# One head's weights moved to ScalarE in every second index unit, layernorm statistics moved to the ends of both attentions, and a wider ring of banks in the second attention

## What is computed

```python
x = x + attn_a(layernorm(x))   # 16 heads, low-rank keys and values, rope, causal, and a top-k index mask
x = x + ffn(layernorm(x))      # 8 routed experts, top 2, and one shared expert
x = x + attn_b(layernorm(x))   # 16 heads of 16, ALiBi, causal
x = x + ffn(layernorm(x))
```

```python
dots = relu(einsum('bqhd,bkhd->bhqk', qi, ki))
index_scores = einsum('bhqk,h->bqk', dots, idx_w)      # weights of the heads, one number each
mask = index_scores >= kth largest of the row          # k from the pooled input
```

## Time and profile before

| | us |
|---|---|
| median of 3 runs | 2647.25 |
| lowest, highest | 2645.97, 2653.23 |
| profiled execution | 2644.66 |
| its span, first to last instruction | 2642.8 |
| PE busy | 2301.2 (87%) |
| DVE busy | 1812.3 (69%) |
| ACT busy | 1667.3 (63%) |
| POOL busy | 721.4 (27%) |

### The profile page before, as it was taken

The page is one execution under the profiler, slowest core; times in us unless marked ns, Lnnn a source line. Parts: engine busy times, 40 slices in busy tenths (PEclk is TensorE's granted clock), DMA queues, the critical chain, the costliest instruction groups (busy, mean ns, idle before and its releaser), DMA issues. The chain is left out here.

```text
span 2642.8 us, 42209 instructions
## 1 busy us (share of the span) xinstructions
PE 2301.2 (87%) x12536; PEld 1570.9 (59%) x12536; DVE 1812.3 (69%) x4044; ACT 1667.3 (63%) x3045; POOL 721.4 (27%) x992
## 2 busy tenths in 40 slices
PE   6956595657999999999999999799589999997995
PEld 3633263346778777877787878465344544444663
DVE  4888788875777677767776777542559888864523
ACT  3779587955777777777777777423226777775232
POOL 0215411542321332133214432136231000000163
PEclk9978797878999999999999999899778999999998
DMA  1011102131000000000000000412360101000124
GB/s 50 1 40 64 64 1 74 56 128 45 22 13 9 26 21 13 9 26 21 13 13 21 21 1 1 129 43 85 108 171 30 50 2 49 2 2 4 53 86 146
DMA packets 77562, 113.17 MB, mean 43 GB/s; under 512 B 23860, under 2 KB 51860, under 8 KB 74644
## 3 DMA queue, kind: packets, MB, share of 16 engines
q1 hardware_dynamic: 66776, 89.55, 10.8%
q0 software_dynamic: 10560, 20.86, 2.6%
HBM read 67.25 MB, written 39.58 MB: 40 GB/s over the span
## 5 line engine op out<-in xcount | busy, mean ns | idle before, releaser
L1425 DVE TENSOR_TENSOR aa_pt_lo<-psum,aa_pt_hi 128x512 fp32r<-128x512 f32 x544 | 350.3, 685 | 82.8 <-ACT aa_pt_hi L1355 80.2
L1900 DVE TENSOR_REDUCE ab_part_max<-psum 128x1 f32<-128x512 f32 (+3 forms) x640 | 348.0, 603 | 68.6 <-PE psum L1746 66.5
L1355 ACT ACTIVATE aa_pt_hi<-psum 128x512 fp32r<-128x512 f32 x544 | 297.2, 597 | 116.1 <-PE psum L1285 113.2
L1412 DVE CUSTOM_DVE_ANT_0 aa_prob<-psum,bias 128x512 f32<-128x512 f32 (+2 forms) x480 | 278.5, 597 | 118.4 <-PE psum L1275 99.9
L1848 ACT ACTIVATE ab_prob<-psum 128x512 f32<-128x512 f32 (+3 forms) x640 | 290.8, 544 | 91.6 <-PE psum L1775 89.0
L1239 POOL TENSOR_TENSOR x<-aa_y_out,x 128x256 f32<-128x256 f32 x256 | 188.3, 735 | 354.9 <-ACT aa_y_out L1373 310.1
L1273 PE MATMUL psum<-ka_hi,aa_q_hi 128*128 128x512 f32 (+3 forms) x640 | 268.6, 420 | 10.9 <-POOL aa_q_lo L1207 8.0
L1285 PE MATMUL psum<-ident,aa_prob 128*128 128x128 f32 x1600 | 253.0, 274 | 5.9 <-issue 4.6
L1347 ACT ACTIVATE aa_prob<-aa_prob,aa_neg_max 128x128 f32<-128x128 f32 (+11 forms) x192 | 227.9, 1188 | 43.3 <-DVE aa_neg_max L1418 41.6
L1296 PE MATMUL psum<-aa_pt_hi,c_stack 128*128 128x512 f32 x544 | 233.9, 430 | 5.9 <-ACT aa_out_t L1362 4.3
L1275 PE MATMUL psum<-ka_hi,aa_q_lo 128*128 128x512 f32 (+3 forms) x640 | 236.9, 370 | 0.0
(11 more groups left out here) (346 smaller groups left out, 4710.1 us busy)
## 6 DMA issues: line engine op xcount, KB each, us to landing
q_rows<-ixt_q_out SPq DMA_DIRECT2D x64, 256.0 KB, 2.0
aa_q_row<-q_rows SPq DMA_DIRECT2D x64, 256.0 KB, 2.6
f_back<-done SPq DMA_DIRECT2D x16, 512.0 KB, 7.8
w<-in_w SPq DMA_DIRECT2D x6, 896.0 KB, 9.8
x<-in_hidden SPq DMA_DIRECT2D x2, 2048.0 KB, 11.5
b_q_stack<-stash_q_hi SPq DMA_DIRECT2D x12, 256.0 KB, 3.8
b_k_stack<-stash_k_hi SPq DMA_DIRECT2D x12, 256.0 KB, 4.4
ixt_wq_n<-in_Wq_nope_T SPq DMA_DIRECT2D x2, 1024.0 KB, 5.1
```

What stands on the lines that cost most here:

```text
L1355: nc.scalar.activation(pt_hi[(TB[t] + j) % RING][:], turn_bank[(TB[t] + j) % RING], ACT.Copy).then_inc(pt_hi_done, 1)
L1412: nc.vector.tensor_tensor_reduce(prob[t % 2][h][:, c * CH:c * CH + w], score_bank[(QB[t] + h * chunks[t] + c) % 2][:, 0:w], bias[:, TRI[t] ...
L1425: nc.vector.tensor_tensor(pt_lo[ring][:], turn_bank[(TB[t] + j) % RING], pt_hi[ring][:].bitcast(F32), ALU.subtract).then_inc(pt_lo_done, 1)
L1900: nc.vector.tensor_reduce(part_max[e % 2][:, at, part:part + 1], s_bank[piece % PIECES][:, 0:w], AX.X, ALU.max).then_inc(s_used, 1)
```

## The change

It has four parts.

In `index_scores`, odd units no longer multiply head 0 on DVE. ACT does it: after the relus of heads 0 and 1 it copies `relu[:, 0, :]`, scaled by the weight, into `scores`, and counts that in the new semaphore `weighed`. DVE starts an odd unit with head 1 and waits there for `weighed`. ACT's relu of head 0 in an even unit waits for its own copy (`weighed`) where it waited for DVE. Even units keep their form, and DVE's sums are counted 7 to a pair of units instead of 8.

At the end of `attention_a` DVE takes the statistics of each tile once POOL has added its last head, and the second layernorm gets them; it loses its own.

In `attention_b` the last transposed scores may use seven banks. Up to the last score nothing changes. From the first slot after it (`FREED`) the slots go round banks 0 to 6; PE waits at that slot until DVE has freed all score banks (`s_used`), and at each slot for what was last in its bank.

Also in `attention_b`, the sixteen reciprocals of the output tiles become one instruction over all tiles, in place, ahead of the first tile, and each tile's statistics are taken one step behind its addition. The fourth layernorm gets them.

```diff
+    DVE_SUMS = 2 * HI - 1
...
+        weighed = sem("weighed")
+
+        def sums(u, h):
+            return DVE_SUMS * (u // 2) + (HI if u % 2 else 1) + h
+
+        def into(u):
+            t, half = divmod(u, HALVES)
+            return scores[:, t, half * WIDE:(half + 1) * WIDE]
...
                 for u in range(UNITS):
                     for h in range(HI):
                         act.wait_ge(dotted, u * HI + h + 1)
-                        if u:
-                            act.wait_ge(summed, (u - 1) * HI + h + 1)
+                        if u % 2 == 0 and u and h == 0:
+                            act.wait_ge(weighed, u // 2)
+                        elif u:
+                            act.wait_ge(summed, sums(u - 1, h))
                         nc.scalar.activation(relu[:, h, :], pair(h), ACT.Relu).then_inc(relu_done, 1)
+                        if u % 2 and h == 1:
+                            act.wait_ge(relu_done, u * HI + 1)
+                            nc.scalar.activation(into(u), relu[:, 0, :], ACT.Copy, scale=weight[:, 0:1]).then_inc(weighed, 1)
                         if u * HI + h in LATER:
                             keep_high(LATER[u * HI + h])
...
                 for u in range(UNITS):
-                    t, half = divmod(u, HALVES)
-                    into = scores[:, t, half * WIDE:(half + 1) * WIDE]
                     for h in range(HI):
-                        dve.wait_ge(relu_done, u * HI + h + 1)
                         if h == 0:
-                            nc.vector.tensor_scalar(into, relu[:, h, :], weight[:, 0:1], None, ALU.mult).then_inc(summed, 1)
+                            if u % 2 == 0:
+                                dve.wait_ge(relu_done, u * HI + 1)
+                                nc.vector.tensor_scalar(into(u), relu[:, 0, :], weight[:, 0:1], None, ALU.mult).then_inc(summed, 1)
                         else:
-                            dve.wait_ge(summed, u * HI + h)
-                            nc.vector.scalar_tensor_tensor(out=into, in0=relu[:, h, :], scalar=weight[:, h:h + 1], in1=into,
+                            dve.wait_ge(relu_done, u * HI + h + 1)
+                            if u % 2 and h == 1:
+                                dve.wait_ge(weighed, u // 2 + 1)
+                            else:
+                                dve.wait_ge(summed, sums(u, h - 1))
+                            nc.vector.scalar_tensor_tensor(out=into(u), in0=relu[:, h, :], scalar=weight[:, h:h + 1], in1=into(u),
                                                            op0=ALU.mult, op1=ALU.add).then_inc(summed, 1)
                         if u * HI + h in LATER:
                             keep_low(LATER[u * HI + h])
...
                 walk(dve, before, run, dve_order)
+                for t in range(NT):
+                    dve.wait_ge(x_added, ((NG - 1) * NT + t + 1) * GH + 4 * GH)
+                    nc.vector.bn_stats(stats[:, t, :], x[:, t, :])
...
+    LAST_S = max(n for n, what in enumerate(STEPS) if what[0] == "s")
+    FREED = min(SLOT[what] for what in STEPS[LAST_S:] if what in SLOT)
+    HOME, LEFT, last_in = [], [], {}
+    for slot in range(SLOTS_USED):
+        home = PIECES + slot % RING if slot < FREED else (slot - FREED) % (PIECES + RING)
+        HOME.append(home)
+        LEFT.append(last_in.get(home, -1) + 1)
+        last_in[home] = slot
...
-        inv = [sb(f"inv{p}", [P, HB, 1]) for p in range(DEEP)]
...
+                def wait_home(slot):
+                    if slot == FREED:
+                        pe.wait_ge(s_used, PIECES_USED)
+                    if LEFT[slot]:
+                        pe.wait_ge(t_taken, LEFT[slot])
...
                 def turn_max(e):
 
                     slot = SLOT[("turn", e)]
                     pe.wait_ge(max_ready, e + 1)
-                    if slot >= RING:
-                        pe.wait_ge(t_taken, slot - RING + 1)
-                    nc.tensor.transpose(t_bank[slot % RING][0:4 * GB, 0:P], row_max[e % 2][:], const["ident"][:]).then_inc(t_ready, 1)
+                    wait_home(slot)
+                    nc.tensor.transpose(bank[HOME[slot]][0:4 * GB, 0:P], row_max[e % 2][:], const["ident"][:]).then_inc(t_ready, 1)
...
                 dve.wait_ge(t_taken, SLOTS_USED)
-                for t in range(NT + LATE):
+                nc.vector.reciprocal(o_sums[:, :, :, DHB:], o_sums[:, :, :, DHB:]).then_inc(inv_done, 1)
+                dve.wait_ge(inv_done, 1)
+                for t in range(NT + LATE + 1):
                     p = t % DEEP
-                    if t < NT:
-                        nc.vector.reciprocal(inv[p][:], o_sums[:, t, :, DHB:]).then_inc(inv_done, 1)
-                    if t >= LATE:
+                    if LATE <= t < NT + LATE:
                         dve.wait_ge(out_done, t - LATE + 1)
                         nc.vector.tensor_tensor(x[:, t - LATE, :], x[:, t - LATE, :], out_bank[(t - LATE) % DEEP][:, 0:D],
                                                 ALU.add).then_inc(x_done, 1)
                     if t < NT:
-                        dve.wait_ge(inv_done, t + 1)
                         if t >= DEEP:
                             dve.wait_ge(o_turned, t - DEEP + 1)
                         nc.vector.tensor_tensor(o[p].rearrange("p (h d) -> p h d", d=DHB), o_sums[:, t, :, 0:DHB],
-                                                inv[p][:].to_broadcast([P, HB, DHB]), ALU.mult).then_inc(o_done, 1)
+                                                o_sums[:, t, :, DHB:].to_broadcast([P, HB, DHB]), ALU.mult).then_inc(o_done, 1)
+                    if t > LATE:
+                        dve.wait_ge(x_done, t - LATE)
+                        nc.vector.bn_stats(stats[:, t - LATE - 1, :], x[:, t - LATE - 1, :])
...
-            layernorm(nc, "ln2", x, xT, bank, const["ident"], mean, rstd, xn, router["gate_w"], router_in[0], bank[7], load)
+            layernorm(nc, "ln2", x, xT, bank, const["ident"], mean, rstd, xn, router["gate_w"], router_in[0], bank[7], load, stats)
...
-            layernorm(nc, "ln4", x, xT, bank, const["ident"], mean, rstd, xn, router["gate_w"], router_in[1], bank[7], load)
+            layernorm(nc, "ln4", x, xT, bank, const["ident"], mean, rstd, xn, router["gate_w"], router_in[1], bank[7], load, stats)
```

More of the change, by code:

```diff
@@ L1761, in transposed_score @@
                     w, slot = (c + 1) * CH - q0, SLOT[("t", i, h)]
-                    out, at = t_bank[slot % RING], slice(base(h), base(h) + R_MAX + 1)
+                    out, at = bank[HOME[slot]], slice(base(h), base(h) + R_MAX + 1)
                     q, k = q_stack[g % 2][h // 2], k_stack[g % 2][h // 2]
@@ L1796, in flip @@
                     pe.wait_ge(kept, e + 1)
-                    pe.wait_ge(t_taken, slot - RING + 1)
+                    wait_home(slot)
                     for j in range(CH // P):
-                        last = nc.tensor.transpose(t_bank[slot % RING][:, j * P:(j + 1) * P], o_rows[e % 2][:, j * P:(j + 1) * P],
+                        last = nc.tensor.transpose(bank[HOME[slot]][:, j * P:(j + 1) * P], o_rows[e % 2][:, j * P:(j + 1) * P],
                                                    const["ident"][:])
@@ L1847, in exponential @@
                         act.wait_ge(pv_done, i - 1)
-                    nc.scalar.activation(prob[i % 2][h][:, 0:w], t_bank[slot % RING][:, 0:w], ACT.Exp).then_inc(t_taken, 1)
+                    nc.scalar.activation(prob[i % 2][h][:, 0:w], bank[HOME[slot]][:, 0:w], ACT.Exp).then_inc(t_taken, 1)
                 def negate(e):
@@ L1855, in negate @@
                         act.wait_ge(max_in[e % 2], e // 2 * GB * 16)
-                    nc.scalar.activation(neg_max[e % 2][:], t_bank[slot % RING][0:4 * GB, 0:P], ACT.Copy,
+                    nc.scalar.activation(neg_max[e % 2][:], bank[HOME[slot]][0:4 * GB, 0:P], ACT.Copy,
                                          scale=-1.0).then_inc(t_taken, 1)
```

17 lines of the change are left out of this document (8 added, 9 removed).

## The result

The changed kernel takes 2626.15 us (median of 4 runs, 2623.76 to 2627.00); the kernel before took 2646.90 beside it. The ratio is 0.9913, with a 95% interval of 0.9901 to 0.9924: of 2647.25 us that is 2624 us, where 2633 was forecast. The profiled span fell from 2642.8 to 2625.2 us.

What follows compares the result with a forecast made beforehand. Bounds: DVE in index scores from the seventh unit, ACT in the last exponentials, PE in output tiles. Terms -6.6 - 4.7 + 1.1 - 3.9 = -14.1 us took the median from 2647.25 to 2633.1 us; range 2625 to 2643.

Steps and rivals of the forecast that it cites:

- the index stages: Two index score stages: moving head 0's multiply to ACT in odd units gives -3.5 and -3.1, together -6.6 us.
- the tiles: Output tiles of attention b: one reciprocal of 1.6 us ahead of the first tile, +1.05 us net.
- the ring: Last scores of attention b: PE waits 1.54 us for DVE's last maxima, 0.48 comes back, +1.1 us.
- all copies hidden: Rival, index stages: ACT's early units have room, gain 14.4 us instead of 6.6, median 2625.3; chance 0.12.
- delay at the seventh unit: Index stages: copies in the first six units, where ACT is late, bring the seventh unit 1.65 us later.
- ACT bounds: Rival, index stages: ACT becomes the bound, index gain is nil, median 2639.7; chance 0.20.
- End of attention a, layernorm two: Statistics leave the layernorm, -5.60 us, and lengthen attention a's block end, +0.9; together -4.7 us.
- +0.65: End of attention b: the last two statistics stick out behind the last output addition, +0.65 us.
- -5.59: Layernorm four: it loses its statistics, forecast at -5.60 us.
- clock rival: Rival, attention b's end: PE's lower clock holds after the ring's wait, 33 us lost, 2666 us; chance 0.03.

Runs made afterwards that it cites:

- f2: Kernel before with the index_scores edit alone, plus a tiny DVE multiply in place of each multiply moved to ACT; ratio 0.9973, attention a 1033.09 us.
- h1 to h3: Kernel before with only padding at attention a's start: 16, 64, or 32 tiny DVE multiplies, the last with 16 ACT copies; ratios 0.9990, 0.9989, 0.9997.
- h3: Kernel before with only 32 tiny DVE multiplies and 16 tiny ACT copies at attention a's start; ratio 0.9997, attention a 1035.95 us.
- f4: Kernel before with the index_scores edit alone, ACT's copies only in odd units from the seventh on; ratio 0.9936.
- g2: Kernel before with the output tile and layernorm four edits alone, reciprocals of all but the last sixteen elements taken ahead of the last sums; ratio 0.9981.
- g3: Changed kernel with copies from unit 7 on, score banks joining behind the last transpose of maxima, and early reciprocals, against the kernel before; ratio 0.9883.

## Why the prediction was right and wrong

**The sum failed at a step that it did not contain.** I costed attention a at nothing, because nothing in it was edited. It gained 5.2 us and, run again, 5.5. Of the 5.2, 2.1 came in the third quarters of the looped groups: the engines' gaps moved because the programs ahead are sixteen instructions shorter or longer, shown by padding that undoes it (f2, which leaves 0.3 of it) and padding that does it alone (h1 to h3). Another 3.0 came at the loop's turns, where the lower clock ended sooner. That is seen and not explained, and it is the larger part: in the kernels with the index part the turns are 1.1 to 3.7 us shorter than before, f2 included, whose DVE program has its old length. Without those 5.2 us the profiled execution would have gained 12.4, against 14.1 forecast, and the median would have been some 2629, inside the range. So the range, too, left out that unedited stretches move by some us when the program ahead of them changes. That the sum missed by only 3.1 us is partly luck: against the forecast the index stages gave 3.6 us less and the tiles 1.5 less, attention a 5.2 more and the ring 2.2 more. The rival "all copies hidden" (2625.3) lies nearest to the measured time by chance; the index stages gave 3.0 us and not 14.4.

**Index stages: mechanism right, -6.6 became -3.0.** DVE's pair of units, the early waits for the copy, multiplies in even units only: as described. Three terms were off. (1) The delay at the seventh unit, put at 1.65 us, was 2.2 in both stages of the index part alone and 2.17 in the second stage of the changed kernel. I let the first copy go free and counted one wait; all three copies are waited for, for 1.2, 1.9 and 1.6 us. (2) In the first stage of the changed kernel it was 3.6: 1.4 more, absent in the index part alone and in the changed kernel run again, so scatter; h3, whose index stages are those of before, shows 1.5 more at the same place (34.91). (3) Three of the five pairs take 8.95 us, not 8.81, and from the seventh unit to the threshold the index part alone gained 4.6 and 4.2 us, not 5.1 and 4.8. When the first multiply of the odd unit went, the 0.14 by which one of DVE's two multiplies in a pair was longer stayed, on another instruction. The rival "ACT bounds" put the same place in question and had the wrong end: ACT is late in the first six units, and DVE waits for none of its copies after them.

The Trainium skill (ScalarE: Activation LUTs, "Rules for kernel authors") gives multiplies to VectorE. ACT's 1.14 us against DVE's 0.75 agree with it on the price, and the index part alone disagrees with it on the result: DVE was the late engine, and the two stages gained 4.4 us. In units 1, 3 and 5, where ACT was late, the rule was right (f4).

**End of attention a, layernorm two: right.** -5.60, and +0.42 in place of +0.9: the block's end on DVE instead of POOL cost nothing beyond the last statistics themselves.

**Ring: the wait right to 0.06 us, its return wrong.** I read 44 exponentials in 22.06 us as "without a gap" from a merged row. Between them lay waits for PE too short to split it, 1.7 us with the visible ones (27.02 us from the sums ahead to the last four exponentials became 25.31). Another 0.7 came back between negation and the exponentials behind the DMA. -2.6 instead of -0.5. Of that some 1 us is the clock: the mean behind the negation was 0.95 where it had been 0.92, and kernels with the ring of four gained 1.0 to 1.3 us there in the same way.

**Output tiles: +2.6 and, again, +3.7, instead of +1.05.** The reciprocal was 1.76 us, not 1.6: 6.3 ns for each of the 240 elements behind the first sixteen (0.25 us), 5.7 taken. At like clocks the edit costs 0.9 to 1.4 us, which fits the forecast. What I left out is PE's clock at this place: my own rival on it lay at the negation, but the lower clock at the tiles cost 1.3 us in the changed kernel and 2.0 when run again. The edit lengthens PE's idle time there from 1.32 to 2.83 us; whether that brings or lengthens the lower clock is open, since it came in several kernels without the edit. The tile's period of 1.09 us held, statistics included, as did +0.65 and -5.59.

The Trainium skill (VectorE: DVE Perf Modes, "First, the fixed hardware budget") has the divide step repeated eight times; the estimate of 2.1 us plus the start is above the 1.76 measured, and the slope of 6.3 ns lies between it and the one I took.

**The clock rival (2666 us)** did not come: behind the negation and at the tiles PE's lower clock ended within some 7 us each time it came.

## What to carry to other kernels

Move work to the other engine only where the one that gives is late, unit by unit: the first units of a pipeline can have another bound than the rest, and three misplaced copies cost half of what five good ones gain. A merged row says nothing of waits shorter than its threshold; compare count over time with the mean by form before calling a stretch gapless. And leave room, some 3 to 5 us of 2600 here, for stretches that are not edited: program length ahead of a loop and PE's clock after an idle moment move them.

## What the runs showed of the hardware that was not expected

- With sixteen instructions of no use (128x1 multiplies) ahead of a loop it was 3.3 us shorter (1036.5 to 1033.3), 1.4 of it in the stretches that a gap had left. Gaps of 0.27 to 0.45 us sit at a place of the program that moves with the instructions ahead.
- A scaled copy from SBUF to SBUF on ACT takes 1.14 us for 128x1024, an unscaled one 1.05.
- A reciprocal on DVE takes 0.25, 0.46, 1.35 and 1.76 us for 16, 48, 192 and 256 elements per partition, 6.2 to 6.6 ns for each added element.
- PE idle for 1.04 us ahead of the output tiles was followed by matmuls at the lower clock in one kernel (1.92 us, g2) and at a granted clock of 1.00 in another (1.13 us, g3).
